# Moving steps between places in four engines' orders of an fp32 AdaLN block with a mixture of experts

## The chip, the cores and the metric

The kernel runs on one core of a Trainium2 chip. The metric is the device time of one execution in microseconds (us), as the median of several runs of the same program.

## The reference, cut to what matters

Input x has 2 x 2048 tokens (4096 in all) of D = 512 numbers in fp32. Six rows per sequence (shift, scale and gain of either half) come from c and wmod.

```python
h = layernorm(x) * (1 + ca) + sa
qkv = rms(h) @ w_qkv.T;  q, k = rms(q), rms(k);  w = exp(k)
y = sigmoid(q) * cumsum(w * v) / (cumsum(w) + 1e-6)
u, g = split(y @ w_swiglu.T)
x = x + ga * (h + (u * silu(g)) @ w_out.T)
h = layernorm(x) * (1 + cb) + sb
gates = softmax over the 2 largest of the 8 logits h @ gate_w
routed = sum over the 2 experts: gate * (gelu(h @ w1[e] + b1[e]) @ w2[e] + b2[e])
shared = gelu(h @ shared_w1 + shared_b1) @ shared_w2 + shared_b2
x = x + gb * (routed + shared)
```

The gains ga and gb are first corrected: sign kept, absolute value at least 0.25.

## The kernel before

Tokens are taken in 8 tiles of 512 (`NT`, the last is `LAST`) and 32 groups of 128 (`NG`). Every fp32 product is made of three matmuls: each operand is split into a high and a low part, and high x high, low x high and high x low are added in one bank (L697 to L699 for products with columns of x, L702 to L704 for those by tokens). The order of the work on each engine is written out by hand, engine by engine: a block for SyncE (L363), GpSimd (L604), TensorE (L695), ScalarE (L1053) and VectorE (L1373). They are held together by semaphores that count.

The stages are, in order:

- **First stage** (to about 366 us): for each group, normalise it, turn it, project it to q, k and v, and add up the running sums. The transposes of w, e and k times v are in `sums` (L754, L761 for w); ahead of the first of them, in group 1, TensorE waits for both shift rows (`shift_ok`, L799). ScalarE writes the shift row in `take_shift` (L1108) out of a bank in which the product with wmod (L716) left it; that of sequence 1 is called in group 1, behind the columns' high parts (L1205). ScalarE's exponentials are at L1158, the spreads' seeds at L1127.
- **Pass b** (366 to about 905 us) and **pass c** (to about 1456 us): two halves of the SwiGLU. Per tile there are 8 blocks s. Block s makes two first products from the columns of x (`up2`, 24 matmuls), VectorE multiplies their results into s_t (L1622), ScalarE rounds its high part (L1239), VectorE makes the low part s_lo (L1625), and `down` adds the second product of an earlier block (12 matmuls). In tile 0 of pass b weight pieces are split along the way; VectorE's part of a piece is `piece_lo` (L1411, L1418). VectorE also computes the residual there: `token_stats` (L1628) for a tile, `first_residual` (L1668) for each of its four groups, with gain rows that `rows_for_b` (L1654) makes ready for a sequence: the correction of the gain `fix_gain` (L1647, four instructions) and two products.
- **Shared expert** (1456 to about 1676 us): per tile 4 first products of 12 matmuls (`up1`, L820), 4 second ones of 12 (`down`, L836), written as `shared_tile` (L989). Its input, the columns xs of the second norm, comes from DRAM in halves of a tile, 1 MB each, into three buffers: `load_half` (L518) waits by `half_left` (L511) until the half that held the buffer has been used. For an even one that is the second chunk of the last first product (`xs_free`), for an odd one the last chunk. `second_norm_out(LAST)` (L480) stores the four h rows of the last tile and its residual, and then loads r_t for tile 0. `evacuate_s` (L1925) on VectorE adds a tile's second products, times the gain, to r_t (L1684 and L1688), which comes from DRAM over SyncE's queue at L439. In tiles 0 and 1 the last tile's h rows are also turned (`rows_to_hT`, L864, transposes at L869) and VectorE takes their low parts in `hT_lo` (L1872, L1874).
- **Routed experts** (1677 us to the end): 71 slots of 128 token rows, sorted by expert. Per slot TensorE turns the rows, makes a first and a second product, GpSimd gathers rows and scatters results. VectorE's last step of a slot is `slot_o` (L2008): gb_row (the gain of the slot's tokens) and, behind it, o_t = bank x gate x gb_row. Right ahead of `slot_o` stands a register load with the number of a later slot's expert (`expert`, L2004).

## Time and profile before

| | us |
|---|---|
| median of 3 runs | 1939.67 |
| lowest and highest | 1938.92, 1943.29 |
| profiled execution, device time | 1936.98 |
| profiled execution, span of the trace | 1935.2 |
| TensorE busy | 1893.0 |
| VectorE busy | 1279.0 |
| ScalarE busy | 650.1 |
| GpSimd busy | 284.7 |

The profile is of one execution, its times are from the start of its span. The mean granted clock of TensorE was 0.995 of the full one. The page has the busy time of each engine and 40 slices of the span; the trace behind it has each instruction with its start, its length, the idle time of its engine before it, and what ended that idle time.

### The profile page before, as it was taken

The numbers are of one execution on the slowest core, as the hardware profiler recorded it, in microseconds if no ns is written. First come the engines' busy times: TensorE is split into PE (matmuls) and PEld (weight loads), VectorE is DVE, ScalarE is ACT, GpSimd is POOL, SyncE is SP. The second block draws the span as 40 slices with busy tenths as digits, with TensorE's granted clock in tenths as the row PEclk, the third lists the DMA queues.
The fourth block names the chain that finished last, engine by engine and source line by source line (L and its number), as shares of the span: only waits on it lengthen the run. The fifth ranks groups of instructions, "written<-read, shape, count | busy, mean of one in ns | idle before, by whom it ended". The sixth has DMA issues, their size and how long they took to land.

```text
span 1935.2 us, 26114 instructions
## 1 busy us (share of the span) xinstructions
PE 1893.0 (98%) x8882; PEld 1536.5 (79%) x8882; DVE 1279.0 (66%) x2639; ACT 650.1 (34%) x1309; POOL 284.7 (15%) x251
## 2 busy tenths in 40 slices
PE   7999999999999999999999999999998999999998
PEld 4688888878888888888888888888886777788886
DVE  6789999875545554556356456557556565599997
ACT  4677776621111111123112212222222332344443
POOL 0000000000000000000001011011020230388885
PEclk9999999999999999999999999999998999999999
DMA  5313112321110211025012422312344776588886
GB/s 189 135 49 104 54 50 66 131 78 64 66 56 10 77 66 44 22 90 182 23 65 82 116 68 82 138 68 82 116 133 183 249 227 216 180 156 154 153 153 97
DMA packets 88990, 206.74 MB, mean 107 GB/s; under 512 B 9781, under 2 KB 26454, under 8 KB 81772
## 3 DMA queue, kind: packets, MB, share of 16 engines
q1 hardware_dynamic: 65292, 144.55, 21.8%
q0 software_dynamic: 23568, 60.51, 14.7%
q8 instruction: 74, 1.21, 0.3%
q14 instruction: 56, 0.46, 0.1%
HBM read 126.95 MB, written 80.51 MB: 107 GB/s over the span
## 4 chain that ended last, share of the span: by engine, by line
PE 81%; POOL 8%; issue 4%; DVE 4%; DMA 3%; ACT 1%; POOLq 0%; SPq 0%; DVEq 0%; ACTq 0%
PE bank L697 13%; PE bank L699 13%; PE bank L698 13%; PE bank L702 12%; PE bank L704 11%; PE bank L703 11%; POOL out L661 5%; POOL rows_t L651 3%; DMA xs<-columns 2%; PE bank L716 1%; PE bank L731 1%; PE bank L761 1%; PE bank L772 1%; PE bank L765 1%; PE bank L869 1%
## 5 line engine op out<-in xcount | busy, mean ns | idle before, releaser
L697 PE MATMUL bank<-x_hi,w_blk 128*128 128x512 f32 x1024 | 403.2, 394 | 3.4 <-DVE s_t L1622 2.3
L699 PE MATMUL bank<-x_hi,w_blk 128*128 128x512 f32 x1024 | 399.5, 390 | 0.0
L698 PE MATMUL bank<-x_lo,w_blk 128*128 128x512 f32 x1024 | 399.2, 390 | 0.0
L1622 DVE TENSOR_TENSOR s_t<-act_t,bank 128x512 f32<-128x512 f32 x128 | 87.9, 687 | 272.7 <-PE bank L699 259.1
L1239 ACT ACTIVATE s_hi<-s_t 128x512 fp32r<-128x512 f32 x128 | 80.9, 632 | 436.2 <-DVE s_t L1622 417.3
L697 PEld LDWEIGHTS bank<-x_hi,w_blk 128*128 128x128 f32 x1024 | 192.7, 188 | 43.1 <-DVE w_blk L1418 2.7
L699 PEld LDWEIGHTS bank<-x_hi,w_blk 128*128 128x128 f32 x1024 | 192.6, 188 | 40.8
L698 PEld LDWEIGHTS bank<-x_lo,w_blk 128*128 128x128 f32 x1024 | 192.7, 188 | 38.9
L702 PE MATMUL bank<-w_blk,s_hi 128*128 128x512 f32 x512 | 199.9, 390 | 0.0
L704 PE MATMUL bank<-w_blk,s_lo 128*128 128x512 f32 x512 | 199.4, 390 | 0.0
L703 PE MATMUL bank<-w_blk,s_hi 128*128 128x512 f32 x512 | 199.3, 389 | 0.0
L1237 ACT ACTIVATE act_t<-bank 128x512 f32<-128x512 f32 x128 | 76.4, 596 | 353.4 <-PE bank L699 349.7
L702 PE MATMUL bank<-w_blk,xc_hi 128*128 128x512 f32 x384 | 156.6, 408 | 3.6 <-DVE xc_lo L1488 2.8
L704 PE MATMUL bank<-w_blk,xc_lo 128*128 128x512 f32 x384 | 150.6, 392 | 0.0
L703 PE MATMUL bank<-w_blk,xc_hi 128*128 128x512 f32 x384 | 149.8, 390 | 0.0
L1625 DVE TENSOR_TENSOR s_lo<-s_t,s_hi 128x512 fp32r<-128x512 f32 x128 | 88.7, 693 | 89.4 <-ACT s_hi L1239 86.6
L608 POOL DMA_DIRECT2D raw<-w_swi x16 | 8.7, 546 | 895.6 <-DVE w_blk L1418 810.9
L623 POOL DMA_INDIRECT slot_list<-pay,pos x64 | 65.0, 1016 | 463.4 <-DVE pos L1758 446.0
L661 POOL DMA_INDIRECT out<-o_t,ids_t x71 | 112.9, 1590 | 42.4 <-DVE o_t L2024 20.1
L702 PEld LDWEIGHTS bank<-w_blk,s_hi 128*128 128x128 f32 x512 | 96.1, 188 | 20.5
L704 PEld LDWEIGHTS bank<-w_blk,s_lo 128*128 128x128 f32 x512 | 96.1, 188 | 20.2
L703 PEld LDWEIGHTS bank<-w_blk,s_hi 128*128 128x128 f32 x512 | 96.1, 188 | 19.9
(272 smaller groups left out, 3445.1 us busy)
## 6 DMA issues: line engine op xcount, KB each, us to landing
x_t<-y_scratch SPq DMA_DIRECT2D x16, 1024.0 KB, 5.1
residual<-r_t SPq DMA_DIRECT2D x16, 1024.0 KB, 4.3
r_t<-residual SPq DMA_DIRECT2D x16, 1024.0 KB
columns<-hT SPq DMA_DIRECT2D x16, 1024.0 KB, 6.3
xs<-columns SPq DMA_DIRECT2D x16, 1024.0 KB, 8.7
raw<-w_swi POOLq DMA_DIRECT2D x16, 768.0 KB, 4.4
y_scratch<-y_t SPq DMA_DIRECT2D x32, 256.0 KB, 2.7
r_t<-x_tok SPq DMA_DIRECT2D x8, 1024.0 KB
```

Source lines behind the costliest of these rows:

```text
L623: pool.indirect_dma_start(list_dram, bass.IndirectOffsetOnAxis(ap=pos[:, 2 * s + k:2 * s + k + 1], axis=0), pay[:, s, k, :], None).then_in ...
L661: pool.indirect_dma_start(out, bass.IndirectOffsetOnAxis(ap=ids_t[:, j:j + 1], axis=0), o_t[j % NO][:, :], None, compute_op=ALU.add).then_ ...
L697: nc.tensor.matmul(dst, w[:, 0, col:col + P], rhs_hi, start=start, stop=False)
L698: nc.tensor.matmul(dst, w[:, 0, col:col + P], rhs_lo, start=False, stop=False)
L699: return nc.tensor.matmul(dst, w[:, 1, col:col + P], rhs_hi, start=False, stop=stop)
L702: nc.tensor.matmul(dst, lhs_hi, w[:, 0, col:col + D], start=start, stop=False)
L703: nc.tensor.matmul(dst, lhs_hi, w[:, 1, col:col + D], start=False, stop=False)
L704: return nc.tensor.matmul(dst, lhs_lo, w[:, 0, col:col + D], start=False, stop=stop)
L1237: nc.scalar.activation(act_t[:, s % 2, :], bank[4 + 2 * s % 3][:, :], ACT.Silu).then_inc(f.act_ok, 1)
L1239: nc.scalar.activation(s_hi[:, s % 3, :], s_t[:, s % 2, :], ACT.Copy).then_inc(f.sh_ok, 1)
L1622: nc.vector.tensor_tensor(s_t[:, s % 2, :], act_t[:, s % 2, :], bank[4 + (2 * s + 1) % 3][:, :], ALU.mult).then_inc(f.s_ok, 1)
L1625: nc.vector.tensor_tensor(s_lo[:, s % 3, :], s_t[:, s % 2, :], s_hi[:, s % 3, :].bitcast(F32), ALU.subtract).then_inc(f.sl_ok, 1)
```

## The change

1. ScalarE: `take_shift(1)` goes from group 1 to group 0, right behind the second exponential.
2. VectorE, pass b: `rows_for_b(0)` goes from block 2 of tile 0 to block 1 and corrects only the gain of sequence 0. The gain of sequence 1 is corrected in `rows_for_b(1)`, in tile 4. The token statistics and the residuals of tile 0 go one block later; those of the other tiles stay.
3. SyncE: half 3 is loaded ahead of the last tile's `second_norm_out`, and half 2t + 2 at the start of tile t.
4. TensorE: the four first products of a shared tile go ahead of its second ones. Of these, 0 and 1 follow first product 3, then 2 and 3 in the steps behind.
5. VectorE, routed slots: gb_row is written in `slot_gain`, at the end of the slot before, into two buffers (those of p_t), where it waits for o_t of two slots earlier.

```diff
--- before.py
+++ after.py
@@ -161,10 +161,11 @@
         NR = len(rows_t)
         o_t = [at(f"o_t{i}", k, [P, D]) for i, k in enumerate((180, 164, 166, 168, 170, 182, 128, 130, 132, 134))]
         NO = len(o_t)
-        gb_row = at("gb_row", 174, [P, D])
         gT_hi = at("gT_hi", 184, [P, 2, H], F32R)
         gT_lo = at("gT_lo", 186, [P, 2, H], F32R)
         p_t = [at(f"p_t{i}", 188 + 2 * i, [P, D]) for i in range(2)]
+
+        gb_row = p_t
         late_rows = [o_t[0], o_t[5], p_t[0], p_t[1]]
         u_t = at("u_t", 200, [P, 2, H])
         gl_t = at("gl_t", 202, [P, 2, H])
@@ -556,8 +557,12 @@
             sp.wait_ge(ffn["c"].ev_ok, NSUB * NT)
             sp.dma_start(b2_raw[:, :], b2p).then_inc(b_in, 16)
             gates_in(0)
+            load_half(3)
             second_norm_out(LAST)
             for t in range(NT):
+                if 0 < t < LAST:
+
+                    load_half(2 * t + 2)
                 if t == 1:
                     hT_out(LAST)
                 if t == 4:
@@ -570,11 +575,9 @@
                     load_gain(1)
                 if t + 1 < NT:
                     gates_in(t + 1)
-                if t < LAST:
-                    if t > 0:
-                        load_half(2 * t + 2)
+                if 0 < t < LAST:
                     load_half(2 * t + 3)
-                else:
+                if t == LAST:
                     half_left(2 * LAST - 2)
                     sp.dma_start(b1r_t[:, :], b1r).then_inc(b_in, 16)
                 sp.wait_ge(ffn["s"].ev_ok, NSUB * (t + 1))
@@ -995,8 +998,9 @@
                         pe.wait_ge(ffn["s"].act_ok, NB_S * NT)
                         slot_rows(0)
                         slot_rows(1)
-                    if s >= 2:
-                        down("s", t, s - 2, w_shr[:, s - 2, :, :], QKV_W, NB_S)
+
+                    for d in {3: (0, 1), 4: (2,), 5: (3,)}.get(s, ()):
+                        down("s", t, d, w_shr[:, d, :, :], QKV_W, NB_S)
                     if (t, s) == (0, 1):
                         logits_to_tokens(LAST - 1)
                     if (t, s) == (1, 3):
@@ -1202,8 +1206,6 @@
                     for n in range(1, NSUB):
                         square_h(n)
                     seed_root(0)
-                if g == 1:
-                    take_shift(1)
                 if g in A_TURNS:
                     piece_hi(B0 + A_TURNS.index(g))
 
@@ -1221,6 +1223,7 @@
                 exponential(g, 0, w_t)
                 exponential(g, 1, e_t)
                 if g == 0:
+                    take_shift(1)
                     seed_spread(1)
                 if g >= 1:
                     reciprocal(g - 1)
@@ -1653,9 +1656,7 @@
 
             def rows_for_b(q):
                 dve.wait_ge(bc_in, 16 * (4 if q == 0 else 6))
-                if q == 0:
-                    fix_gain(ga_t[0], tmp[0])
-                    fix_gain(ga_t[1], tmp[1])
+                fix_gain(ga_t[q], tmp[0])
                 then(nc.vector.tensor_tensor(a1_t[:, :], a1_t[:, :], ga_t[q][:, :], ALU.mult))
                 then(nc.vector.tensor_tensor(b1_t[:, :], b1_t[:, :], ga_t[q][:, :], ALU.mult))
 
@@ -1884,16 +1885,19 @@
                             if t == 0 and s == 0:
                                 denominator(NG - 1)
                                 sum_kv(NG - 1)
+                            if t == 0 and s == 1:
+                                rows_for_b(0)
                             if t == 0 and s == 2:
                                 quotient(NG - 1)
-                                rows_for_b(0)
                             if t == T_SEQ and s == 2:
                                 rows_for_b(1)
-                            if s == 2:
+
+                            first = 3 if t == 0 else 2
+                            if s == first:
                                 dve.wait_ge(r_in, 16 * (t + 1))
                                 token_stats()
-                            if 3 <= s < 3 + NSUB:
-                                first_residual(t, s - 3)
+                            if first < s <= first + NSUB:
+                                first_residual(t, s - first - 1)
                             if t == 0 and s == 7:
                                 nc.vector.memset(prev[:, :, :], 0.0)
                                 gate_weights()
@@ -2005,12 +2009,18 @@
 
                 return dve.value_load(tab[0:1, 1, j:j + 1], min_val=0, max_val=(E - 1) * H)
 
+            def slot_gain(j):
+
+                if j >= 2:
+                    dve.wait_ge(rt.o_ok, j - 1)
+                if j < 2:
+
+                    dve.wait_ge(ffn["s"].ev_ok, NSUB * LAST + 3 + j)
+                nc.vector.scalar_tensor_tensor(out=gb_row[j % 2][:, :], in0=gbd_t[:, :], scalar=late_t[:, j:j + 1],
+                                               in1=gbs_t[0][:, :], op0=ALU.mult, op1=ALU.add).then_inc(rt.gr_ok, 1)
+
             def slot_o(j):
 
-                if j >= 1:
-                    dve.wait_ge(rt.o_ok, j)
-                nc.vector.scalar_tensor_tensor(out=gb_row[:, :], in0=gbd_t[:, :], scalar=late_t[:, j:j + 1],
-                                               in1=gbs_t[0][:, :], op0=ALU.mult, op1=ALU.add).then_inc(rt.gr_ok, 1)
                 dve.wait_ge(rt.gr_ok, j + 1)
                 dve.wait_ge(rt.dn, j + 1)
                 if j == 1:
@@ -2022,7 +2032,7 @@
                 if j >= NO:
                     dve.wait_ge(sc_st[(j - NO) % NA], 16 * ((j - NO) // NA + 2))
                 nc.vector.scalar_tensor_tensor(out=o_t[j % NO][:, :], in0=bank_o[j % 2][:, :], scalar=gate_t[:, j:j + 1],
-                                               in1=gb_row[:, :], op0=ALU.mult, op1=ALU.mult).then_inc(rt.o_ok, 1)
+                                               in1=gb_row[j % 2][:, :], op0=ALU.mult, op1=ALU.mult).then_inc(rt.o_ok, 1)
 
 
             dve.wait_ge(b_in, 32)
@@ -2052,6 +2062,7 @@
                     slot_g(j + 1)
                 if j in R_TURNS:
                     piece_lo(R0 + 14 + R_TURNS.index(j))
+                slot_gain(j)
             slot_o(NSLOT - 1)
```

SyncE's queue between pass c and tile 2 of the shared expert; xs_89 to xs_91 are the three buffers of halves. Before:

```order
170 L504 DMA graw<-gate_rows 40x512
171 L484 DMA h_rows<-hrow 128x512 x4
172 L486 DMA residual<-r_t 128x4x512
173 L439 DMA r_t<-residual 128x4x512
174 L504 DMA graw<-gate_rows 40x512
175 L527 DMA xs_89<-columns 128x2048
176 L581 DMA out<-r_t 128x4x512
177 L439 DMA r_t<-residual 128x4x512
178 L509 DMA columns<-hT 128x2048 x2
179 L504 DMA graw<-gate_rows 40x512
180 L527 DMA xs_90<-columns 128x2048
181 L527 DMA xs_91<-columns 128x2048
```

In the change:

```order
170 L505 DMA graw<-gate_rows 40x512
171 L528 DMA xs_89<-columns 128x2048
172 L485 DMA h_rows<-hrow 128x512 x4
173 L487 DMA residual<-r_t 128x4x512
174 L440 DMA r_t<-residual 128x4x512
175 L505 DMA graw<-gate_rows 40x512
176 L584 DMA out<-r_t 128x4x512
177 L440 DMA r_t<-residual 128x4x512
178 L528 DMA xs_90<-columns 128x2048
179 L510 DMA columns<-hT 128x2048 x2
180 L505 DMA graw<-gate_rows 40x512
181 L528 DMA xs_91<-columns 128x2048
```

Half 3 (xs_89) now stands ahead of the four h rows and the residual, and half 4 (xs_90) ahead of the columns of the last tile.

VectorE in tile 0 of pass b, from the low part of block 0 on. Before:

```order
662 L1622 TENSOR_TENSOR s_t<-act_t,bank 128x512
663 L1625 TENSOR_TENSOR s_lo<-s_t,s_hi 128x512
664 L1418 TENSOR_TENSOR w_blk<-raw_83,w_blk 128x1536
665 L1622 TENSOR_TENSOR s_t<-act_t,bank 128x512
666 L1625 TENSOR_TENSOR s_lo<-s_t,s_hi 128x512
667 L1554 TENSOR_TENSOR den_t_59<-den_t_59,rec_t 128x512
668 L1555 TENSOR_TENSOR y_t_62<-kv_sum_57,rec_t 128x512
669 L1556 SCALAR_TENSOR_TENSOR y_t_62<-den_t_59,y_t_62 128x512
670 L1648 TENSOR_SCALAR tmp_114<-ga_t_110 128x512
671 L1649 TENSOR_SCALAR tmp_114<-tmp_114 128x512
672 L1650 TENSOR_TENSOR ga_t_110<-ga_t_110,tmp_114 128x512
673 L1651 SCALAR_TENSOR_TENSOR ga_t_110<-ga_t_110,tmp_114 128x512
```

In the change:

```order
662 L1625 TENSOR_TENSOR s_t<-act_t,bank 128x512
663 L1628 TENSOR_TENSOR s_lo<-s_t,s_hi 128x512
664 L1651 TENSOR_SCALAR tmp_114<-ga_t_110 128x512
665 L1652 TENSOR_SCALAR tmp_114<-tmp_114 128x512
666 L1653 TENSOR_TENSOR ga_t_110<-ga_t_110,tmp_114 128x512
667 L1654 SCALAR_TENSOR_TENSOR ga_t_110<-ga_t_110,tmp_114 128x512
668 L1660 TENSOR_TENSOR a_t<-a_t,ga_t_110 128x512
669 L1661 TENSOR_TENSOR b_t<-b_t,ga_t_110 128x512
670 L1421 TENSOR_TENSOR w_blk<-raw_83,w_blk 128x1536
671 L1625 TENSOR_TENSOR s_t<-act_t,bank 128x512
672 L1628 TENSOR_TENSOR s_lo<-s_t,s_hi 128x512
673 L1557 TENSOR_TENSOR den_t_59<-den_t_59,rec_t 128x512
```

One correction of the gain and the two products now stand ahead of the weight piece, and the second correction is gone from here.

TensorE in tile 0 of the shared expert, from the end of first product 2 (xs) on; the rows of L702 and further with w_shr first are second product 0. Before:

```order
6040 L698 MATMUL bank<-xs_90,w_shr 128x512
6041 L699 MATMUL bank<-xs_90,w_shr 128x512
6042 L702 MATMUL bank<-w_shr,s_hi 128x512
6043 L703 MATMUL bank<-w_shr,s_hi 128x512
6044 L704 MATMUL bank<-w_shr,s_lo 128x512
```

In the change (all lines are three further on, L700 to L702 is a first product):

```order
6040 L701 MATMUL bank<-xs_90,w_shr 128x512
6041 L702 MATMUL bank<-xs_90,w_shr 128x512
6042 L700 MATMUL bank<-xs_89,w_shr 128x512
6043 L701 MATMUL bank<-xs_89,w_shr 128x512
6044 L702 MATMUL bank<-xs_89,w_shr 128x512
```

First product 3 now follows at once, and second product 0 comes behind it.

## Rows read from the trace of the kernel before

**Rows 1.** The page: busy time of TensorE, granted clock by slice.
```profile
PE 1893.0 (98%) x8882; PEld 1536.5 (79%) x8882; DVE 1279.0 (66%) x2639; ACT 650.1 (34%) x1309; POOL 284.7 (15%) x251
...
PEclk9999999999999999999999999999998999999999
```

**Rows 2.** Timeline of TensorE: five rows with idle time before them.
```profile
46.13 0.63 PE L761 MATMUL bank<-ident_t,w_t 128*128 128x128 f32 x4 [3.25 <-issue]
...
405.25 0.47 PE L697 MATMUL bank<-x_hi,w_blk 128*128 128x512 f32 x1 [2.28 <-DVE s_t L1622]
...
1493.56 0.80 PE L697 MATMUL bank<-xs,w_shr 128*128 128x512 f32 x1 [7.74 <-DMA xs<-columns]
...
1551.79 0.50 PE L697 MATMUL bank<-xs,w_shr 128*128 128x512 f32 x1 [1.56 <-DMA xs<-columns]
...
1578.45 0.50 PE L697 MATMUL bank<-xs,w_shr 128*128 128x512 f32 x1 [1.37 <-DMA xs<-columns]
```

**Rows 3.** Timeline of ScalarE, 39 to 55 us.
```profile
39.70 0.68 ACT L1158 ACTIVATE e_t<-bank,rk_a 128x512 f32<-128x512 f32 x1
...
42.12 0.20 ACT L1127 ACTIVATE sv_a<-va_a 128x4 f32<-128x4 f32 x1 [1.73 <-DVE va_a L1439]
...
45.44 0.59 ACT L1110 ACTIVATE shift_a<-bank 128x512 f32<-128x512 f32 x1
...
53.96 0.59 ACT L1184 ACTIVATE wmod_t<-bank 2x512 f32<-2x512 f32 x1 [0.42 <-PE bank L716]
```

**Rows 4.** Timeline of VectorE, 385 to 405 us.
```profile
385.65 1.76 DVE L1418 TENSOR_TENSOR w_blk<-raw,w_blk 128x1536 fp32r<-128x1536 f32 x1 [4.81 <-ACT w_blk L1106]
...
391.25 0.42 DVE L1648 TENSOR_SCALAR tmp<-ga_t 128x512 f32<-128x512 f32 x1
...
396.72 0.69 DVE L1660 TENSOR_TENSOR b_t<-b_t,ga_t 128x512 f32<-128x512 f32 x1
...
402.75 1.76 DVE L1418 TENSOR_TENSOR w_blk<-raw,w_blk 128x1536 fp32r<-128x1536 f32 x1
404.43 0.68 DVE L1622 TENSOR_TENSOR s_t<-act_t,bank 128x512 f32<-128x512 f32 x1
```

**Rows 5.** Chain of waits, 405 to 408 us: start, length, what.
```profile
405.72 0.23 PE bank L698
...
406.88 0.43 PE bank L699
```

**Rows 6.** Timeline of all engines, 1468 to 1501 us (SPq is SyncE's queue).
```profile
1468.67 0.39 PE L697 MATMUL bank<-xs,w_shr 128*128 128x512 f32 x1
...
1484.18 0.47 PE L697 MATMUL bank<-xs,w_shr 128*128 128x512 f32 x1
...
1485.22 0.37 SPq L439 DMA_DIRECT2D r_t<-residual  x1
...
1491.16 1.29 DVE L1684 TENSOR_TENSOR tmp<-bank,gbs_t 128x512 f32<-128x512 f32 x2 [3.13 <-DMA r_t<-residual]
...
1498.51 0.68 DVE L1874 TENSOR_TENSOR hT<-bank,hT 128x512 fp32r<-128x512 f32 x1
...
1500.55 0.60 PE L869 MATMUL bank<-ident_t,hrow 128*128 128x128 f32 x4
```

**Rows 7.** The page's DMA issues: name, queue, operation, count, KB, us to landing.
```profile
x_t<-y_scratch SPq DMA_DIRECT2D x16, 1024.0 KB, 5.1
residual<-r_t SPq DMA_DIRECT2D x16, 1024.0 KB, 4.3
```

**Rows 8.** Chain of waits, the longest pieces: start, length, what.
```profile
1563.00 15.41 DMA xs<-columns
```

**Rows 9.** Routed slots: timeline of VectorE, then gb_row's instructions (ns min/median/max).
```profile
1687.84 0.75 DVE L2012 SCALAR_TENSOR_TENSOR gb_row<-gbd_t,late_t,gbs_t 128x512 f32<-128x512 f32 x1 [0.99 <-issue]
...
L2012 DVE SCALAR_TENSOR_TENSOR gb_row<-gbd_t,late_t,gbs_t x71: 742/752/779, 1687.8 to 1925.8; 128x512 f32<-128x512 f32 x71
```

**Rows 10.** Busy us of the engines, 1700 to 1800 us, by engine.
```profile
1700.00:1800.00 100.00, 99.41 (x575) 85.39 (x575) 94.61 (x177) 40.31 (x87) 80.92 (x60) 1.00 0.87 156
```

## Prediction of the change, made before it was run

> **What bounds the kernel now.** I read the busy line and the slices of the page first. TensorE is busy for 1893.0 of 1935.2 us and its clock reads 9 in all slices but one [rows 1]. So the time is TensorE's own work plus some 42 us without any, and an edit pays only where it fills one of those gaps. I then went through TensorE's timeline for rows with an idle time before them. Five matter [rows 2]: 3.25 us at 46.13, 2.28 us at 405.25, and 7.74, 1.56 and 1.37 us in the shared expert. The edits touch all five, and none removes a matmul.
>
> A gap can cost more than its length. Behind the one at 405.25 the chain of waits shows matmuls at 0.43 us each where the ones before take 0.23 [rows 5]: the granted clock has fallen to the lower of its levels, 1.2 instead of 2.4 GHz. Seven such rows follow, and two that are partly slow: 7 x 0.20 + 0.2 = 1.6 us. Behind the gap at 1493.56 I count eight, a first matmul 0.3 us too long and four transposes 0.4 us too long: 2.3 us. Behind the 3.25 us gap at 46.13 there is none.
>
> **The shift row (ScalarE).** The gap at 46.13 is the transposes of the first group's w, which stand behind a wait for shift_ok. ScalarE wrote that row at 45.44, behind group 1's first square and columns, though its product was done long before. In the change it stands behind the second exponential (39.70 + 0.68), in 1.73 us in which ScalarE was idle [rows 3], so it costs nothing there and is ready at 41. The gap goes whole. A little comes back: the copy at 53.96 [rows 3] waited for TensorE by 0.42 us, and group 3's transposes wait for that copy; with TensorE 3.25 us earlier it is ScalarE's own chain that is late, by about 0.25. I take 3.0 us, between 2.5 (if VectorE lags too) and 3.3.
>
> **The gain rows (VectorE, first pass, tile 0).** The gap at 405.25 waits for s_t of block 3, which came at 404.43. In front of it VectorE ran the two corrections of the gain and the two products from 391.25 to 397.41 and the token statistics from there to 402.75, then a weight piece of 1.76 us [rows 4]. Ten instructions in 6.2 us: one correction (four of them) is 2.4 us, the two products 1.4. Now one correction and the products run behind block 1, where VectorE waited 4.81 us for the piece at 385.65; 3.8 fits. The statistics go behind block 3's products, so VectorE is free for s_t of block 3 at 391.25 + 1.76 = 393.0, and TensorE needs it at 402.97 (405.25 - 2.28). What is late next is block 4. If block 3's product is done one block (36 matmuls of 0.23, 8.3 us) behind 387.3, at 395.6, VectorE is through with it at 397.7, with the statistics (5.3) at 403.0 and with the piece at 404.8; s_t of block 4 is needed a block behind 402.97, at 411. The other correction, 2.4 us, moves to tile 4, where 48 matmuls (10.9 us) lie between the product it delays and the one that needs it; that cover would have to shrink by more than half. So the gap and its slow matmuls go: 2.28 + 1.6 = 3.9 us. Bounds: 2.3 if a slow stretch comes up elsewhere, 4.0 if all goes.
> The Trainium skill, TensorE: Matmul & The Clock Gate, section Why this matters for your kernels, warns only of idle gaps longer than this one. By it the gap would not have cost clock, this term would be 2.3 and the sum 10.3. The trace disagrees: the 0.43 us matmuls are there, so the row decides.
>
> **The halves of columns (SyncE) and the order of products.** Half 3, which tile 1 needs in its third chunk, was issued right behind r_t's load of 1485.22, at the end of a chain of h rows and the residual's store; it was waited for until 1493.56 [rows 2, 6]. Now half 3 stands before that chain and waits only for the first two chunks of tile 0's last first product. That product began at 1468.67 [rows 6] and moves forward by one second product (12 matmuls, 2.7 us), so half 3 leaves at about 1467.4, before the first h row's store, and is in place long before 1484.
> The 7.74 us are still not won. In tile 1 TensorE runs product 0, four transposes and product 1 (2.7 + 0.5 + 2.7 from 1484.18, so to 1490.1), and then the transposes of the last h row, which wait until VectorE has taken the third low half hT (L1874). On VectorE that stands behind the eviction of tile 0, which waits for r_t. Before, r_t was issued at 1485.22 and the eviction ran from 1491.16 in four pairs of 1.29, to 1496.30 [rows 6]. Without half 3 beside it a 1 MB load took 5.1 us [rows 7], so the eviction runs 1490.3 to 1495.5; s_lo and hT add 1.3, and TensorE goes on at 1496.8. The xs wait of 7.74 becomes an hT wait of 6.7. Those transposes ran at 1500.55 before [rows 6], so 3.75 us are won, and since a gap of this size slowed the matmuls behind it, 2.0 (between the 1.6 and the 2.3 counted) go back: 1.8 us. Bounds: 4.6 if the clock holds and r_t lands as fast as a store [rows 7], 0.7 if r_t lands no sooner (2.95 won, 2.3 given back).
> The two gaps of 1.56 and 1.37 wait for halves 7 and 9, which took 15.4 us to land; one of the two rows stands in [rows 8]. Both were issued right behind their even half. Now the even halves go 2 and 4 us earlier, half 7 leaves 2.2 us earlier (its wait ends with the product that moved) and half 9 0.8 us earlier, with less in front of it. The first gap goes even at 15.4 us; of the second at most 0.6 stays. I take 2.7 of 2.9, bounds 1.5 and 2.9.
> The Trainium skill, DMA: Bandwidth & Descriptors, section Issuing engines are not separate DMA queues, says that all transfers interleave on the same 16 engines. By it, issuing in another order frees nothing, half 9 lands 0.8 us earlier and no more, and the sum is 11.3. No row of before shows the halves apart.
> Moving the second products back costs nothing by itself: the same matmuls run in a tile, the eviction of the tile before gets one product more, and the third s_hi now waits for product 0 of the second kind, with 5.4 us to go before it is used.
>
> **The row of gb (VectorE, routed slots).** It is written behind slot_g, in front of the register load, into two buffers. The ops and their order on VectorE stay. One idle of 0.99 us stood in front of the first such row [rows 9]; later slots have no such idle. I take 0.5 us, half of it, bounds 0 and 1.1 (all of it, and 0.1 elsewhere).
>
> **Sum.** 3.0 + 3.9 + 1.8 + 2.7 + 0.5 = 11.9. The profiled execution took 1936.98 us, so it becomes 1925.1. The median of the runs shown stands 2.7 above it, so the forecast is 1939.67 - 11.9 = 1927.8. The bounds add up to 7.0 and 15.9.
>
> **Rivals.**
> Nothing takes the place of the long xs wait. Then 3.0 + 3.9 + 7.7 + 2.3 + 2.9 + 0.5 = 20.3, or 1919.4. For it: the page names xs alone as that gap's releaser. Against it: the program order above. 7%.
> The shared expert gives nothing: the hT wait and its slow matmuls eat the first term, and the halves land no sooner, since something other than the halves before them holds the DMA engines. For it: 15.4 us against 5.1 for the same 1 MB [rows 7, 8] is more than one half beside another explains. Left are 3.0 + 3.9 + 0.5 = 7.4, or 1932.3. 17%.
> The gains of the first two places are lost again further on, through a wait that the later start of a load leaves where it was. All work behind them goes by TensorE and no such wait stands in the trace, so: about 1938, 6%.
> Slower: the register load now stands between the gb row and the product that uses it. If VectorE stalls there in every slot, as it did once for 0.99 us, o_t is late in all 71. A slot takes 238.0 / 70 = 3.40 us and VectorE is free for 5.4% of it, 0.18 us [rows 9, 10], so a stall of 0.5 us costs 0.32 x 71 = 23 us, or 1950.8. It decides the sign from 0.18 + 11.9 / 71 = 0.35 us per slot. Against it: in steady slots the load already stands in front of the gb row, and no idle is seen. 4%.
>
> **Numbers.** The forecast case has 66%. Its own ends are 1939.67 - 15.9 = 1923.8 and 1939.67 - 7.0 = 1932.7; reaching towards the first rival, and over the second, I put the range at 1920 to 1933. About 0.2%, 3.9 us, is what a measurement of this kernel can tell from no change. Faster by more: 66 + 7 + 17 = 90%; within: 6%; slower: 4%.
>
> **What would show it.** No gap before the first w transposes and none before block 5's first product; L697's xs waits gone or under 0.6 us; a new idle of 6 to 7 us in tile 1 in front of the h row's transposes (L869 of before) that ends with hT on VectorE or a load of r_t, with slow matmuls behind it; DMA issue of half 3 about 18 us earlier. If that new idle is missing, I am too high by up to 8 us; if slots take more than 3.5 us each, the rival on the slower side holds; if the halves 7 and 9 are still waited for, it is the second rival.

## The result, and the profile after

| | before | changed |
|---|---|---|
| median of 17 runs each, us | 1940.42 | 1931.22 |
| lowest and highest | 1935.32, 1943.29 | 1929.45, 1934.53 |
| ratio to before, 95% interval | | 0.9956 (0.9950 to 0.9963) |
| profiled execution, device time | 1936.98 | 1933.81 |
| profiled execution, span | 1935.2 | 1932.0 |

The changed kernel is faster by 9.2 us in the medians; the ratio makes it 8.5 us, 7.2 to 9.7. The forecast was 11.9 less, and 1927.8; the measured time is 3.4 us above it.

The page of the changed kernel: TensorE is as busy as before [rows 1], and the median half of columns takes 9.1 us to land (8.7 in the trace of before).

```profile
PE 1895.2 (98%) x8882; PEld 1540.3 (80%) x8882; DVE 1275.1 (66%) x2639; ACT 649.6 (34%) x1309; POOL 281.6 (15%) x251
...
xs<-columns SPq DMA_DIRECT2D x16, 1024.0 KB, 9.1
```

The timeline of TensorE of the changed kernel: the rows that mark the stages, the two longest idle times, and one row behind each of these. The start is first, then the length.

```profile
34.77 0.50 PE L705 MATMUL bank<-w_blk,xc_hi 128*128 128x512 f32 x1 [1.41 <-DVE xc_lo L1491]
...
365.51 0.47 PE L700 MATMUL bank<-x_hi,w_blk 128*128 128x512 f32 x1 [1.01 <-issue]
...
1451.99 0.39 PE L700 MATMUL bank<-xs,w_shr 128*128 128x512 f32 x1
...
1492.80 1.09 PE L872 MATMUL bank<-ident_t,hrow 128*128 128x128 f32 x4 [7.02 <-DVE hT L1875]
...
1493.53 0.78 PE L700 MATMUL bank<-xs,w_shr 128*128 128x512 f32 x1
...
1567.99 0.50 PE L700 MATMUL bank<-xs,w_shr 128*128 128x512 f32 x1
...
1573.69 0.79 PE L700 MATMUL bank<-xs,w_shr 128*128 128x512 f32 x1 [4.05 <-DMA xs<-columns]
...
1574.71 0.63 PE L702 MATMUL bank<-xs,w_shr 128*128 128x512 f32 x1
...
1673.40 0.50 PE L954 MATMUL bank<-w_all,xT_hi 128*128 x1
```

The gap before the first transposes of w and the one before block 5's first product [rows 2] are gone: no idle of 0.6 us or more stands between 42.41 and 365.51, and none of 0.5 us from 366 to 460. Half 3's wait is gone too, and a wait for hT of 7.02 us stands in tile 1 in its place. Half 7's is gone. Half 9 is waited for by 4.05 us, where it was 1.37, and 11 matmuls behind it are spaced 0.43 us instead of 0.23.

Four such rows cut the span into stages (the fourth mark, the first product on w_all, is where the routed experts begin). The marks are the first product that waits 1.41 us for xc_lo (34.77), the first product of pass b (365.51), the first one on xs (1451.99), the first one on w_all (1673.40), and the end of the span. For tiles 1, 3 and 4 of the shared expert the table has their own times, each from the tile's first product (1567.99 for tile 4) to the next tile's. The same cuts in every profiled execution, in us:

| kernel | mark 1 at | first stage | b and c | shared | of it tiles 1, 3, 4 | routed |
|---|---|---|---|---|---|---|
| before | 32.22 | 333.78 | 1090.59 | 219.21 | 37.96, 26.84, 25.98 | 259.4 |
| before, second profile | 32.96 | 336.48 | 1089.01 | 218.26 | 37.75, 27.01, 24.99 | 259.3 |
| changed | 34.77 | 330.74 | 1086.48 | 221.41 | 36.99, 24.97, 31.25 | 258.6 |
| shift row back | 34.70 | 335.40 | 1086.47 | 220.54 | 36.31, 24.98, 30.94 | 258.4 |
| gain rows back | 32.21 | 330.75 | 1090.61 | 222.27 | 36.62, 24.98, 32.41 | 258.2 |
| even halves back | 34.83 | 330.73 | 1086.49 | 221.09 | 36.98, 26.18, 29.71 | 258.5 |
| second products back | 33.08 | 330.76 | 1086.47 | 220.34 | 37.48, 24.99, 29.53 | 258.6 |
| gb row back | 34.45 | 330.74 | 1086.44 | 221.51 | 36.89, 24.98, 31.42 | 259.3 |
| hT early | 32.90 | 330.74 | 1086.44 | 222.53 | 31.03, 24.97, 29.54 | 258.2 |
| lists late | 32.32 | 330.75 | 1086.46 | 227.16 | 37.26, 24.98, 36.59 | 258.4 |
| even halves earlier | 32.37 | 330.75 | 1086.45 | 218.10 | 37.21, 24.98, 27.68 | 258.5 |
| shared part as before | 32.02 | 330.77 | 1086.49 | 217.97 | 37.87, 26.68, 24.99 | 258.7 |
| four more moves | 32.84 | 330.76 | 1086.50 | 209.32 | 31.03, 24.97, 25.00 | 258.2 |
| s_lo first | 34.76 | 330.74 | 1086.42 | 210.23 | 31.75, 24.98, 25.27 | 258.5 |

Where the gaps of [rows 2] are gone, the first stage and passes b and c take the same time to 0.1 us in every execution (330.75; 1086.5). What differs is the start, whose instructions no edit changed (32.0 to 34.8 us to the first mark), and whatever stands behind a gap.

Between the rows of before and of the changed kernel the stages moved by -3.04, -4.11, +2.20 and -0.8 us, in sum -5.75. So the shared expert, from which I had expected 4.5 us, became slower in the profiled execution. The two profiled executions are 3.2 us apart (1936.98 and 1933.81) and not 5.75, since that of the changed kernel came to its first mark 2.55 us later; it was also 2.6 us slower than its kernel's median, and that of before 3.4 us faster than its own.

### The profile page after: what moved, and what is told of

Read it like the earlier page. It is cut to its first block, busy times and chain, and to the rows that moved or that the text cites. A ratio compares the mean times of both kernels' runs of the same rounds, so it can differ in the third digit from the quotient of the medians.

```text
span 1932.0 us, 26114 instructions
## 1 busy us (share of the span) xinstructions
PE 1895.2 (98%) x8882; PEld 1540.3 (80%) x8882; DVE 1275.1 (66%) x2639; ACT 649.6 (34%) x1309; POOL 281.6 (15%) x251
## 4 chain that ended last, share of the span: by engine, by line
PE 83%; POOL 7%; DVE 3%; issue 3%; DMA 3%; ACT 1%; POOLq 0%; SPq 0%; DVEq 0%; ACTq 0%
PE bank L700 13%; PE bank L702 13%; PE bank L701 13%; PE bank L705 12%; PE bank L707 11%; PE bank L706 11%; POOL out L664 4%; POOL rows_t L654 3%; PE bank L719 1%; DMA out<-o_t,ids_t 1%; DMA xs<-columns 1%; PE bank L954 1%; PE bank L734 1%; PE bank L768 1%; PE bank L775 1%
## 5 line engine op out<-in xcount | busy, mean ns | idle before, releaser
L700 PE MATMUL bank<-x_hi,w_blk 128*128 128x512 f32 x1024 | 403.2, 394 | 1.1 <-issue 1.0
L702 PE MATMUL bank<-x_hi,w_blk 128*128 128x512 f32 x1024 | 399.4, 390 | 0.0
L702 PEld LDWEIGHTS bank<-x_hi,w_blk 128*128 128x128 f32 x1024 | 192.4, 188 | 40.4
L700 PEld LDWEIGHTS bank<-x_hi,w_blk 128*128 128x128 f32 x1024 | 192.5, 188 | 40.2 <-issue 1.4
```

The lines of the kernel that those rows point to most:

```text
L700: nc.tensor.matmul(dst, w[:, 0, col:col + P], rhs_hi, start=start, stop=False)
L702: return nc.tensor.matmul(dst, w[:, 1, col:col + P], rhs_hi, start=False, stop=stop)
```

## The experiments

All but one of them start from the changed kernel. The ratios are to the kernel before, with 95% intervals; that of the changed kernel is 0.9950 to 0.9963. Line numbers are those of each kernel.

### The kernel before once more

No edit; one more profiled execution.

> The kernel before, unchanged, for a second profiled execution. The first one began with matmuls at the full clock (32.2 us at a mark that others of these kernels pass at 32.2 to 34.8) and had no slow matmuls behind the 3.25 us gap at 46; the changed kernel with the shift row put back had both the late start and 1.6 us of slow matmuls behind that gap. Theory (whether such a gap costs clock differs from execution to execution): where this execution starts late, its first stage takes 335.4 us from that mark as that kernel's did, else 333.8. The shared expert's waits for halves 7 and 9 differ by under 1 us from 1.56 and 1.37. Rival (the kernel before never loses clock there): 333.8 us either way, and the difference of 9.2 us between the medians against 5.75 us between the traces stays open.

Measured: 1937.85 us. Its timeline of TensorE, the same marks and gaps:

```profile
32.96 0.50 PE L702 MATMUL bank<-w_blk,xc_hi 128*128 128x512 f32 x1 [1.41 <-DVE xc_lo L1488]
...
46.87 1.08 PE L761 MATMUL bank<-ident_t,w_t 128*128 128x128 f32 x4 [3.26 <-issue]
...
50.32 0.63 PE L704 MATMUL bank<-w_blk,xc_lo 128*128 128x512 f32 x1
...
369.44 0.47 PE L697 MATMUL bank<-x_hi,w_blk 128*128 128x512 f32 x1 [1.01 <-issue]
...
408.73 0.47 PE L697 MATMUL bank<-x_hi,w_blk 128*128 128x512 f32 x1 [2.28 <-DVE s_t L1622]
...
409.03 0.39 PE L698 MATMUL bank<-x_lo,w_blk 128*128 128x512 f32 x1
...
1553.64 0.49 PE L697 MATMUL bank<-xs,w_shr 128*128 128x512 f32 x1 [1.72 <-DMA xs<-columns]
1553.98 0.39 PE L698 MATMUL bank<-xs,w_shr 128*128 128x512 f32 x1
```

The same gap of 3.26 us is followed by ten slow rows, at the lower of the two clock levels (three groups of transposes at 1.06 to 1.08 us instead of 0.6, one matmul at 0.78 and six at 0.63), at a granted clock of 0.77 over the stretch from 45 to 60 us, where it was 1.00 in the first profile. The windows view of this execution (stretch, its length, busy time of PE, PEld, DVE, ACT and POOL, granted clock, DMA share, GB/s):

```profile
45.00:60.00 15.00, 13.13 (x44) 8.60 (x45) 10.54 (x21) 7.98 (x21) 0.00 (x0) 0.77 0.45 169
```

The first stage takes 336.48 us. And the same gap of 2.28 us at block 5 is here followed by matmuls at full speed, where seven slow ones stood [rows 5]. So neither theory nor rival had it whole: the clock behind a gap differs from execution to execution, but not with the start (this one was at 32.96, near the early end), and the price behind the first gap was 2.7 us (336.48 - 333.78). Half 9 is waited for by only 0.18 us here, 1.2 less than in the first profile, and half 7 by 1.72 us, with matmuls at full speed behind it.

### The shift row back in group 1

```diff
+                if g == 1:
+                    take_shift(1)
                 if g in A_TURNS:
...
                 if g == 0:
-                    take_shift(1)
                     seed_spread(1)
```

> The changed kernel with the shift row's copy put back into group 1. Theory (a gap at one place that nothing else covers): the 3.25 us gap before the first transposes of w is back, with no slow matmuls behind it; the kernel takes 3.0 us more than the changed one, so about 1934.3 where that takes 1931.2 (6 us under the kernel before). Rival (the start of the first stage absorbs it: ScalarE's chain or the loads are late anyway): under 1 us more, 1931 to 1932.

Measured: 1935.59 us median of 12, ratio 0.9980 (0.9970 to 0.9989). Timeline of TensorE:

```profile
34.70 0.50 PE L705 MATMUL bank<-w_blk,xc_hi 128*128 128x512 f32 x1 [1.41 <-DVE xc_lo L1492]
...
48.62 0.63 PE L764 MATMUL bank<-ident_t,w_t 128*128 128x128 f32 x4 [3.26 <-issue]
...
51.37 0.63 PE L705 MATMUL bank<-w_blk,xc_hi 128*128 128x512 f32 x1
...
370.10 0.47 PE L700 MATMUL bank<-x_hi,w_blk 128*128 128x512 f32 x1 [1.01 <-issue]
```

The gap is back at its place, and behind it one matmul of 0.78 us and six of 0.63. The theory had the gap right and the clock wrong: the first stage is 4.65 us longer than with the edit, the median 4.4 us higher. The edit is worth its 3.0 us at least, and on top of them what the clock takes behind the gap: 0, 1.6 and 2.7 us in three profiled executions that have the gap (333.78, 335.40 and 336.48 against 330.75).

### The gain rows back in front of block 3

```diff
-                fix_gain(ga_t[q], tmp[0])
+                if q == 0:
+                    fix_gain(ga_t[0], tmp[0])
+                    fix_gain(ga_t[1], tmp[1])
...
-                            if t == 0 and s == 1:
-                                rows_for_b(0)
                             if t == 0 and s == 2:
                                 quotient(NG - 1)
+                                rows_for_b(0)
...
-                            first = 3 if t == 0 else 2
+                            first = 2
```

> The changed kernel with VectorE's gain rows, both corrections and the token statistics of tile 0 back where they were. Theory: the 2.28 us gap before block 5's first product is back and the matmuls behind it run at the lower clock, so 3.9 us more, about 1935.1. Rival (the clock falls or not independently of this gap): the gap's 2.3 us alone, about 1933.5, and no matmuls of 0.43 us behind the gap.

Measured: 1934.89 us median of 11, ratio 0.9974 (0.9964 to 0.9984). Timeline of TensorE, the gap and the first of seven slow rows:

```profile
402.23 0.47 PE L700 MATMUL bank<-x_hi,w_blk 128*128 128x512 f32 x1 [2.29 <-DVE s_t L1625]
...
403.15 0.63 PE L700 MATMUL bank<-x_hi,w_blk 128*128 128x512 f32 x1
```

Passes b and c take 4.13 us more, 2.29 of gap and 1.84 of slow matmuls; the median is 3.7 us higher (in this execution half 9 is also waited for by 6.32 us, which makes its shared expert 0.9 us longer). The theory holds in this execution, and in the second one of the kernel before the rival's size does (2.54 us).

### The even halves back, half 3 alone forward

```diff
-                if 0 < t < LAST:
-                    load_half(2 * t + 2)
...
                 if 0 < t < LAST:
+                    load_half(2 * t + 2)
                     load_half(2 * t + 3)
```

> The changed kernel with the even halves 2t+2 issued again where they were (right ahead of half 2t+3); half 3 stays in front of the h rows. It tells what made tile 4 wait 4.05 us for half 9, which took 18.7 us to land. Theory A (the early even half crowds half 9: r_t, half 8 and half 9 go out within 3 us): with half 8 2 us later the load of half 9 does not get shorter by that, since the same three transfers still lie beside each other; the wait stays within 1 us of 4.05. Theory B (only the list scatters of GpSimd matter, which now fall into its flight): also no change. Theory C (half 8 in front of half 9 is the whole loss): half 9 lands in 15.4 us or less and the wait falls under 1.5 us, and the kernel gains 3 to 5 us. In any case the first gap of before (half 7, 1.56 us) stays away if the forward move of the products filled it, and comes back at 0.5 to 1.5 us if the earlier even half did.

Measured: 1932.71 us median of 8, ratio 0.9960 (0.9947 to 0.9973), no difference from the changed kernel that shows. Timeline of TensorE:

```profile
1569.26 0.50 PE L698 MATMUL bank<-xs,w_shr 128*128 128x512 f32 x1 [1.12 <-DMA xs<-columns]
...
1574.42 0.50 PE L698 MATMUL bank<-xs,w_shr 128*128 128x512 f32 x1 [3.52 <-DMA xs<-columns]
```

The first row is half 8, late now at the start of tile 4, the second half 9: together 4.64 us. So the early even half is not the loss (theory C falls); theories A and B both allow this result, and the run does not part them. Half 7 is not waited for.

### The second products back between the first ones

```diff
-                    for d in {3: (0, 1), 4: (2,), 5: (3,)}.get(s, ()):
-                        down("s", t, d, w_shr[:, d, :, :], QKV_W, NB_S)
+                    if s >= 2:
+                        down("s", t, s - 2, w_shr[:, s - 2, :, :], QKV_W, NB_S)
```

> The changed kernel with the shared expert's second products back between the first ones; all loads keep their new order. Theory: half 3 now stands ahead of the h rows and is issued one product (2.7 us) later than with the new order, but still in time, so tile 1's wait is again one for hT of 6.7 to 7 us and not one for xs; each odd half leaves 2.7 us later, so waits for halves 7 and 9 come back at about 1 to 5 us each. In sum 1 to 5 us more than the changed kernel, 1932 to 1936. Rival (the SyncE order did nothing without the products): the xs wait of 7.7 us in tile 1 is back with nothing before it and no hT wait, 1935 to 1937.

Measured: 1930.52 us median of 6, ratio 0.9957 (0.9941 to 0.9973), as the changed kernel. Timeline of TensorE:

```profile
1491.24 1.09 PE L872 MATMUL bank<-ident_t,hrow 128*128 128x128 f32 x4 [7.13 <-DVE hT L1875]
...
1571.97 0.79 PE L700 MATMUL bank<-xs,w_shr 128*128 128x512 f32 x1 [3.47 <-DMA xs<-columns]
```

The wait for hT is there as expected, half 7 is in time and half 9 is late by 3.47 us. I had expected 1 to 5 us more, and none shows: the order of products gives nothing beside the early even halves. Half 7 is in time with the products forward alone (the run above) and with the even halves forward alone (this one); either does.

### The gb row back in front of its product

```diff
             def slot_o(j):
 
+                slot_gain(j)
                 dve.wait_ge(rt.gr_ok, j + 1)
...
-                slot_gain(j)
             slot_o(NSLOT - 1)
```

> The changed kernel with the gb row written again in front of its product, behind the register load (it keeps its two buffers). Theory: the edit gives 0.5 to 0.8 us in the first slots and nothing after, so 0.5 to 0.8 us more, about 1932; the slots' period stays at 3.40 us. Rival (it gave a little in every slot, 0.05 us x 71): 3 us or more, above 1934.

Measured: 1934.15 us median of 5, ratio 0.9961 (0.9947 to 0.9974). The interval reaches over the changed kernel's, so the median tells nothing. The stage does: 259.3 us against 258.6. VectorE's timeline of this kernel, two rows:

```profile
1685.02 0.75 DVE L2019 SCALAR_TENSOR_TENSOR p_t<-gbd_t,late_t,gbs_t 128x512 f32<-128x512 f32 x1 [0.76 <-issue]
...
1692.95 0.75 DVE L2019 SCALAR_TENSOR_TENSOR p_t<-gbd_t,late_t,gbs_t 128x512 f32<-128x512 f32 x1 [0.37 <-issue]
```

In the changed kernel neither idle time stands before these rows; the first of them there:

```profile
1684.42 0.74 DVE L2019 SCALAR_TENSOR_TENSOR p_t<-gbd_t,late_t,gbs_t 128x512 f32<-128x512 f32 x1
```

The two add up to 1.1 us, of which the routed stage shows 0.7. The rival (a gain in every slot) falls.

### The third low half hT ahead of the eviction of tile 0

```diff
                 if t == 0:
                     hT_lo(LAST, 0)
                     hT_lo(LAST, 1)
+                    hT_lo(LAST, 2)
...
-                    if (t, s) in ((1, 0), (1, 1)):
-                        hT_lo(LAST, 2 + s)
+                    if (t, s) == (1, 1):
+                        hT_lo(LAST, 3)
```

> The changed kernel with VectorE's third low half of the last tile's columns (hT) taken ahead of the eviction of tile 0, so that it no longer waits for the load of r_t. Theory: the 7.02 us wait of TensorE in tile 1 and the slow matmuls behind it (1.9 us in the two first products, 0.35 us in the transposes) go, 8 to 9 us less, about 1922.7; the eviction, which waits for r_t anyway, is not later, and TensorE next needs it in the second products of tile 1, which in the changed kernel came 8 us behind the transposes: up to 2 us of a new wait there. Rival (the load of r_t is the true bound, and the wait only moves to the second products of tile 1): 2 us or less gained, 1929 to 1931, with a gap of 5 us or more before a second product that ends with the eviction.

Measured: 1933.57 us median of 5, ratio 0.9965 (0.9951 to 0.9979), no gain. Timeline of TensorE:

```profile
1491.35 0.50 PE L705 MATMUL bank<-w_shr,s_hi 128*128 128x512 f32 x1 [1.55 <-DVE s_lo L1926]
...
1495.62 0.50 PE L705 MATMUL bank<-w_shr,s_hi 128*128 128x512 f32 x1 [1.25 <-DVE s_lo L1926]
...
1514.91 0.80 PE L700 MATMUL bank<-xs,w_shr 128*128 128x512 f32 x1 [4.54 <-DMA xs<-columns]
...
1573.93 0.50 PE L700 MATMUL bank<-xs,w_shr 128*128 128x512 f32 x1 [3.32 <-DMA xs<-columns]
```

The wait for hT is gone and tile 1 takes 31.03 us instead of 36.99. But TensorE is then 6 us early at tile 2 and waits 4.54 us for half 5, with slow matmuls behind. SyncE issues half 5 behind the store of tile 0, r_t and two stores of columns, and it left at 1497.92 and was there at 1514.9. Theory and rival both missed this place: not the next second product was late but the next load.

### The last list scatters held until half 9 is there

```diff
                 fetch(i)
+            pool.wait_ge(xs_in[0], 16 * 4)
             to_lists(LAST)
```

> The changed kernel with GpSimd's last list scatters (8 transfers of many small packets) held back until half 9 has landed. Theory B (those scatters slow half 9): half 9 lands in 10 us or less and the 4.05 us wait of tile 4 goes, with the slow matmuls behind it (2.6 us), so 6 us less there, about 1925, if the later lists cost nothing (the table made of them is read in tile 5, with 10 us in hand). Theory A (r_t, half 8 and half 9 crowd each other): half 9 still takes 15 us or more and the wait stays above 2 us.

Measured: 1937.96 us median of 11, ratio 0.9986 (0.9977 to 0.9995), 6.7 us slower than the changed kernel. TensorE's wait for half 9 is gone. Half 9 left at 1553.12, and GpSimd's first scatter, held until it is there, began at 1564.35, so it landed in 11.2 us. The view of the tile xs has the minimum, median and maximum of all halves:

```profile
DMA to landing us min/median/max: 4.7/9.1/13.7
```

```profile
1564.35 1.00 POOL L626 DMA_INDIRECT slot_list<-pay,pos  x1 [16.02 <-DMA xs<-columns]
```

What is late instead stands in VectorE's and TensorE's timelines:

```profile
1583.18 0.42 DVE L1804 TENSOR_TENSOR tab_c<-bank,thr_t 128x256 f32<-128x256 f32 x1 [11.49 <-DMA steps_t<-steps]
```

```profile
1588.65 0.79 PE L706 MATMUL bank<-w_shr,s_hi 128*128 128x512 f32 x1 [8.89 <-DVE s_lo L1927]
```

The constant tables of the routed stage stand behind the scatters on GpSimd's queue. VectorE waits 11.49 us for the last of them, and TensorE 8.89 us for the s_lo behind that wait. So the scatters were worth some 7.5 us of the 18.7 that half 9 took. Theory B holds for the load, but its 10 us or less was too low, and the gain that it forecast went into the tables.

### The even halves still earlier

```diff
-                if 0 < t < LAST:
-                    load_half(2 * t + 2)
...
                 if 0 < t < LAST:
                     load_half(2 * t + 3)
+                if t < LAST - 1:
+                    load_half(2 * t + 4)
```

> The changed kernel with each even half issued right behind the odd half before it, ahead of the wait for the eviction and the store, so 17 to 20 us earlier; its buffer is free by then. Theory A (three transfers at the same time make half 9 late): half 8 is long in place when half 9 goes out, half 9 is issued 2 us earlier; but half 10 now goes out behind it, so half 9 takes 12 to 16 us and the 4.05 us wait falls under 1 us: 4 to 6 us less, about 1926. Theory B (the list scatters alone): half 9 still takes 17 to 19 us, the wait falls only by the 2 us by which it is issued earlier.

Measured: 1927.44 us median of 5, ratio 0.9930 (0.9916 to 0.9943), 3.8 us faster than the changed kernel. Timeline of TensorE:

```profile
1568.67 0.50 PE L699 MATMUL bank<-xs,w_shr 128*128 128x512 f32 x1 [1.16 <-DMA xs<-columns]
...
1585.55 0.50 PE L704 MATMUL bank<-w_shr,s_hi 128*128 128x512 f32 x1 [1.61 <-DVE s_lo L1925]
```

Half 9 is late by 1.16 us with no slow matmuls behind it, though the scatters are beside it as before: it left at 1552.58 and was there at 1568.6, in 16.0 us. That is theory A's upper end; the wait and the gain just miss its numbers (under 1 us, 4 to 6 us). The 1.61 us are new: s_lo behind VectorE, which waits 1.85 us for the constant tables.

### The shared expert as before, the other edits kept

```diff
-            load_half(3)
             second_norm_out(LAST)
...
-                    load_half(2 * t + 2)
...
+                if t < LAST:
+                    if t > 0:
+                        load_half(2 * t + 2)
                     load_half(2 * t + 3)
...
-                    for d in {3: (0, 1), 4: (2,), 5: (3,)}.get(s, ()):
+                    if s >= 2:
```

> The changed kernel with the third and the fourth edit undone: SyncE's order and the shared expert's products as before, the shift row, the gain rows and the gb row as changed. In the traces the shared expert took 219.2 us before and 221.4 us changed. Theory (the two edits as a pair lost time there): the shared expert takes 219 to 220 us, and the kernel 1 to 2 us less than the changed one, 1929 to 1931. Rival (they gained, and the long wait for half 9 comes with the earlier arrival of everything at that place, so it would be there in this kernel too): half 9 is waited for by 4 us or more beside the 7.7 us of half 3, the shared expert takes 223 us or more, and the kernel 1933 to 1936.

Measured: 1932.75 us median of 10 (1927.05 to 1935.03), ratio 0.9958 (0.9946 to 0.9971). Timeline of TensorE:

```profile
1486.18 0.80 PE L698 MATMUL bank<-xs,w_shr 128*128 128x512 f32 x1 [7.69 <-DMA xs<-columns]
...
1544.25 0.50 PE L698 MATMUL bank<-xs,w_shr 128*128 128x512 f32 x1 [1.42 <-DMA xs<-columns]
```

Half 3 and half 7 are late as before, half 9 by 0.22 us only (it took 14.3 us); the shared expert takes 217.97 us. Neither theory's nor rival's time for the kernel came. The profiled execution (1927.80) was near the fastest of ten, so its half 9 may be a lucky one. The traces say that the third and fourth edits lost 3 us in the mean (three executions with the old order 218.0 to 219.2, four with the new one 220.5 to 222.3); the medians can't tell them from nothing, and stand 1.5 us the other way. Neither bears out a gain of 4.5 us.

### Four more moves together

The even halves earlier (half 10 only behind the store of tile 3), half 5 ahead of the store of tile 0, the third hT ahead of the eviction, and the constant tables ahead of the scatters:

```diff
+                if t < LAST - 1 and t != 3:
+                    load_half(2 * t + 4)
+                if t == 0:
+                    load_half(5)
...
                 sp.dma_start(tokens(out, t), r_t[:, :, :]).then_inc(out_st, 16)
+                if t == 3:
+                    load_half(2 * t + 4)
...
+            pool.dma_start(steps_t[:, :, :], steps.rearrange("p (k e) -> p k e", k=2)).then_inc(sc_st[3], 16)
             for i in range(R0 + 6, R0 + 8):
                 fetch(i)
             to_lists(LAST)
...
+                    hT_lo(LAST, 2)
```

> The changed kernel with four more steps moved: even halves right behind the odd ones (half 10 only behind the store of tile 3, half 5 ahead of the store of tile 0), the third low half hT ahead of the eviction of tile 0, and the four small constant tables of GpSimd loaded ahead of the last list scatters. Theory: tile 1 takes 31.0 us as with the early hT alone, tile 2 26.5 (half 5 no longer late), tile 4 24.7 to 26 (half 9 without a second half behind it, VectorE's tables in time), so the shared expert takes 208 to 211 us against 221.4, and the kernel about 1919 to 1921. Rival (the DMA engines are full there, so a transfer brought forward makes another one late): the waits for halves 5 or 9 stay at 2 us or more together, the shared expert takes over 214 us, 1924 or more.

Measured: 1919.63 us median of 5 (1918.85 to 1922.19), ratio 0.9899 (0.9881 to 0.9916): 20.8 us faster than the kernel before, 11.6 faster than the changed one. The shared expert takes 209.32 us. Its only idle rows of 0.8 us or more in the shared expert, beside the 1.02 us of tile 0 that all kernels have:

```profile
1491.39 0.50 PE L707 MATMUL bank<-w_shr,s_hi 128*128 128x512 f32 x1 [1.56 <-DVE s_lo L1928]
...
1495.65 0.50 PE L707 MATMUL bank<-w_shr,s_hi 128*128 128x512 f32 x1 [1.25 <-DVE s_lo L1928]
```

Early hT alone gave nothing and early even halves gave 3.8 us; together with half 5 and the tables they give 11.6. The early hT had uncovered half 5, the early even halves the constant tables. Half 5 and the tables were not moved alone, so their shares are not shown.

### The first two low parts of tile 1 ahead of the eviction

```diff
                     hT_lo(LAST, 2)
+                    block_s(1, 0)
...
+                if t == 0:
+                    block_s(1, 1)
                 dve.wait_ge(f.dn, NB_S * (t + 1))
...
-                    block_s(t, s)
+                    if (t, s) not in ((1, 0), (1, 1)):
+                        block_s(t, s)
```

> The kernel with the four further moves, and VectorE also takes the low parts of tile 1's first two products ahead of the eviction of tile 0 (one of them behind the correction of the gain). It aims at the two waits for s_lo, 1.56 and 1.25 us, that are left in tile 1. Theory: both go, and the third low part becomes the one waited for, since ScalarE makes its product only behind the gates that VectorE computes behind the eviction: 1.2 to 2.8 us less in tile 1 (31.0 to 28.2 or 29.8 us), the kernel 1917 to 1918.5. Rival (the eviction is now later by as much, and the second products wait for it in place of s_lo): tile 1 takes 31 us as before, 1919 to 1920.

Measured: 1922.12 us median of 4 (1919.28 to 1922.58), ratio 0.9898 (0.9881 to 0.9914), no better than the kernel above. Timeline of TensorE:

```profile
1499.77 0.50 PE L707 MATMUL bank<-w_shr,s_hi 128*128 128x512 f32 x1 [1.70 <-DVE s_lo L1928]
...
1500.97 0.63 PE L708 MATMUL bank<-w_shr,s_hi 128*128 128x512 f32 x1
```

The waits of 1.56 and 1.25 us are gone and one of 1.70 us has come, for the third low part, as the theory said. But seven slow matmuls follow it, where the two waits had none, so tile 1 takes 31.75 us instead of 31.03. Here one wait of 1.7 us cost more than two of 2.8 together. The theory's times (28.2 to 29.8 us for tile 1, 1917 to 1918.5 for the kernel) did not come. Half 9 took 15.5 us in this execution and was late by 0.66, so the four moves leave it little room.

## Why the prediction was right or wrong

The direction and the range were right, and so were the terms of the shift row, the gain rows and the gb row. The likeliest case was not right as a whole: of its 11.9 us the shared expert was to give 4.5, 2.2 at least, and in the traces it became slower by 2.2. That the number came near is in part luck. Between the first two profiles the terms give 5.75, which is below the sum's lower bound of 7.0; the medians lie within it because the two early gaps cost the kernel before more than I had priced. Undoing these two edits raised the median by 4.4 and 3.7 us, and with 0.8 for the gb row that is 8.9 of the 9.2: next to nothing is left for the shared expert in the medians either, though they are no finer than some 2 us. By its terms:

- **Shift row, 3.0.** Right: 3.04 us against the first profile of before, the gap gone whole and nothing new late. As a price it was too small in two of three executions. "Behind the 3.25 us gap at 46.13 there is none" was true of one execution; the two others that were profiled with this gap lost 1.6 and 2.7 us of clock there.
- **Gain rows, 3.9.** Right, if 0.1 above its bound: 4.11 us, and nothing late at block 4 or in tile 4. The Trainium skill (TensorE: Matmul & The Clock Gate, section Why this matters for your kernels) warns only of longer idle gaps. That no clock is lost behind this one holds in one of three executions; the other two, and the 1.70 us gap of the last experiment, lost some. And the 3.25 us gap, long enough for its warning, cost no clock in one of three.
- **Half 3, 1.8.** The mechanism was right to 0.3 us: the wait for hT is 7.02 us where I said 6.7. Tile 1 became 0.97 us shorter, within the bounds of 0.7 and 4.6 and near the low one. Its transposes came 3.1 us earlier in the tile and not 3.75, since the eviction began 5.7 us behind the issue of r_t (1480.61 to 1486.31) and not 5.1; and 2.2 us went back in slow matmuls, where I had 2.0.
- **Halves 7 and 9, 2.7.** This is the step that failed: the time that I gave half 9 to land. Half 7 went as said (tile 3 is 1.87 us shorter). Of half 9 I wrote "at most 0.6 stays", "with less in front of it". It is waited for by 4.05 us, and tile 4 is 5.27 us longer. It did leave earlier against TensorE, by 0.6 us (I had 0.8), but took 18.70 us to land instead of 15.41, and that is the whole loss but for 0.2. SyncE's queue and GpSimd's timeline of the changed kernel show what was beside it:

```profile
1552.25 0.37 SPq L440 DMA_DIRECT2D r_t<-residual  x1
1552.72 0.46 SPq L528 DMA_DIRECT2D xs<-columns  x1
...
1554.95 0.49 SPq L528 DMA_DIRECT2D xs<-columns  x1
```

```profile
1552.88 1.00 POOL L626 DMA_INDIRECT slot_list<-pay,pos  x1 [2.40 <-DVE pos L1759]
...
1562.23 0.96 POOL L626 DMA_INDIRECT slot_list<-pay,pos  x1 [0.30 <-issue]
```

And in the chain of waits (start, length, what):

```profile
1554.95 18.70 DMA xs<-columns
```

In the kernel before, the same transfers (the last row is halves 8 and 9):

```profile
1557.67 0.37 SPq L439 DMA_DIRECT2D r_t<-residual  x1
...
1562.17 1.15 SPq L527 DMA_DIRECT2D xs<-columns  x2
```

```profile
1560.33 1.01 POOL L623 DMA_INDIRECT slot_list<-pay,pos  x1 [2.41 <-DVE pos L1758]
```

And the windows view of the changed kernel while half 9 is in flight, then that of before (its last two numbers are the share of time that the DMA engines were busy, and GB/s):

```profile
1555.00:1574.00 19.00, 14.95 (x62) 10.44 (x61) 7.60 (x11) 1.58 (x2) 9.60 (x13) 0.96 0.99 212
```

```profile
1563.00:1578.00 15.00, 14.08 (x58) 9.64 (x56) 4.40 (x7) 2.27 (x3) 9.94 (x12) 1.00 0.84 200
```

I had counted the microseconds by which half 9 leaves earlier and not what would then fly beside it. On the clock it left 8 us earlier and landed 4.8 us earlier (1573.65 against 1578.41, 1563.00 + 15.41 [rows 8]), while TensorE came 7.4 us earlier. The scatters and half 8 stood beside half 9 in the kernel before too: the first scatter began 2.7 us ahead of it there, 2.1 here. What is new is r_t, which left 5.3 us ahead of half 9 there and 2.7 here. In all the profiled executions that have half 9's issue and landing:

| kernels | r_t ahead of half 9 by, us | half 9 lands in, us |
|---|---|---|
| before, its second profile, shared part as before | 5.1 to 5.5 | 14.2 to 15.4 |
| changed, the five with one edit back, hT early | 2.6 to 3.6 | 17.5 to 21.0 |
| even halves earlier, s_lo first (half 8 not beside it) | 2.5 | 15.5 to 16.0 |
| lists late (scatters not beside it) | 3.1 | 11.2 |

So the scatters take the most, some 7.5 us, as the run without them shows, and half 8 some 3. That r_t's nearness is what added the 3.3 us is seen in how the executions fall into groups; no run moved r_t alone, so it stays likely and not shown. The Trainium skill (DMA: Bandwidth & Descriptors, section Issuing engines are not separate DMA queues) says that transfers run on the same 16 DMA engines and interleave, whichever engine started them, and the trace agrees: without GpSimd's scatters SyncE's load lands in 11.2 us. What I drew from it, that another order frees nothing, is not true of the kernel with four more moves, where the same bytes in another order made the waits for columns go. The sum of 11.3 that I gave by it does not follow either: with half 9 only 0.8 us earlier, 2.9 - 0.6 = 2.3 us are left of the term, and the sum is 11.5.
- **gb row, 0.5.** Right: 0.8 us between before and changed, 0.7 when undone. The slower rival (a stall at the register load) did not come.

The terms as measured between the first profiles are 3.04 + 4.11 + 0.97 + (1.87 - 5.27) + 0.8 = 5.5, and the span from the first mark gives 5.75 (the last 0.23 are in tile 7). The medians give 8.5 to 9.2. Part of the difference is seen: both profiles of the kernel before (1936.98 and 1937.85) were faster than its median, and its two early gaps cost between nothing and 2.7 us of clock (the first) or 1.8 (the second). Its times spread over 8 us, those of the changed kernel over 5. That a slower execution of the kernel before has the late start and both slow stretches at once is an inference, since none was profiled. So the rest, about 3 us, stays open.

The second rival ("the shared expert gives nothing", 1932.3) came nearer to the median than the forecast: its time is 1.1 us off, mine 3.4. Its mechanism was there in part: the hT wait and its slow matmuls ate most of the first term, and one of the two halves was still waited for. Its reason, that something other than the halves before them holds the DMA engines, is what the lists late show.

## What to carry to other kernels

Before a load is moved forward, list what else is in flight in its new place; where the DMA engines are nearly always busy (0.99 here), don't count its landing from its issue and an old duration. A wait that is removed shows the next late transfer, so moves can be worth more together than one by one (nothing and 3.8 us alone, 11.6 with two more): read the trace after each and go on before judging. Price a gap of TensorE of 1.7 to 4 us at its own length and, by these runs, at nothing to 2.7 us more, and take more than one profiled execution before saying which.

## What the runs showed of the hardware

- The clock behind a gap is not fixed by the gap. Behind 3.25 us at the same place: none, 7 and 10 slow rows; behind 2.28 us: 7, 7 and none. Behind 1.56 and 1.25 us, 4 us apart: none; behind one of 1.70 in the last experiment: seven, behind one of 1.72 in the second profile of before: none.
- The way to the first mark takes 32.0 to 34.8 us in kernels whose instructions up to there are the same. It falls into two groups: nine executions reach the mark at 32.0 to 33.1 us, five at 34.5 to 34.8, and the mean granted clock of the first 45 us was 1.00 in the nine and 0.96 in the five (the changed kernel's profile among them). The difference is as large as most of the terms here, so one profiled execution can mislead by it, and it may be why medians of 5 runs of this kernel don't resolve 2 us.
- Long stretches without such a gap repeat to 0.1 us: passes b and c take 1086.42 to 1086.50 us in the eleven executions without the 2.28 us gap.
- Indirect scatters on GpSimd's queue slow a load on SyncE's: the same 1 MB half, with r_t and half 8 beside it, landed in 18.7 us with eight of them and in 11.2 us without.
